# One program in place of two looped phases, in an attention and MLP block on one core

## The chip, the cores and the metric

The kernel runs on one core of a Trainium2 chip, in a single launch. The metric is device time in microseconds (us) of one execution. Shorter is better.

## What is computed

The input is 16 sequences of 256 tokens with 256 features, 4096 tokens in all. The reference, cut to what matters:

```python
x = x + layernorm(attention(layernorm(x), W_Q, W_K, W_V, W_O, biases))   # causal, 16 heads of 128
x = x + layernorm(mlp(layernorm(x), gate, up, down))                     # 2048 wide
# mlp: out = (gelu(x @ Wg.T) * (x @ Wu.T)) @ Wd.T
# Wg, Wu, Wd: two 4-bit codes in each word, a table of 16 values, one scale for 32 values
```

Every float32 product is computed as three matmuls of split operands (`hi` is the operand rounded to the matmul's type, `lo` the rest): hi by hi, hi by lo, lo by hi.

## The kernel before

The 4096 tokens are worked on in 8 chunks of 512. There are two phases, each with its own set of five engine programs (a `Block`), its own semaphores and its own SBUF and PSUM tensors: `attention_phase` for all chunks, then `mlp_phase` for all chunks. The second phase's programs begin when all engines have ended the first's. Each chunk's attention result goes through a scratch tensor in HBM (`x1_scratch`) to the MLP phase.

**Attention.** A chunk has 16 steps, one for each head; `step_plan(j)` writes out the order of the work of step j, and every engine walks the same list. In step j TensorE projects q and k of head j+1 (`project`, 6 matmuls of 512 columns each), transposes the probabilities of head j (`pT`, lines 465 to 467), projects v for four heads in every fourth step, multiplies head j-1's z by W_O (`out`, 12 matmuls of 256 columns), computes the scores of head j+1 and z of head j. ScalarE and VectorE take each result out of PSUM, as its hi and its lo part. In step 14 the next chunk's normalised x is transposed (`xT`, line 382), and q, k and scores "of head 16" are those of the next chunk's head 0. The last chunk does this too: its next chunk is the first one of the MLP phase for `xT`, and for q, k and scores there is no use.

The 16 steps are the body of a hardware loop over the chunks on every engine (`Fori`, on TensorE at line 418), so places in semaphore counts are register values:

```python
            with pe.Fori(0, NCH) as c:
                base = c * FPC
                for j, what in order:
```

At the end of the body come z of head 15, the scores of "head 16" and `out` of head 15. VectorE then evacuates the two output banks with the bias added (line 680).

The heads' weights (12.6 MB as hi and lo) stay in SBUF for the whole phase. The MLP weights are unpacked on the side, 6 of 48 pieces in each chunk: ScalarE starts loads of `words` and `scale` (lines 318 and 320), VectorE turns the codes into values (lines 583 to 599), ScalarE and GpSimd split them, and ScalarE stores hi and lo in an HBM scratch (line 308).

**MLP.** At its start SyncE loads the unpacked weights into SBUF (`w4all`, 12.6 MB, 18 transfers from line 842), since the memory was full of attention's. A chunk has 16 steps of 128 hidden columns. The work runs two steps ahead: step j has gate and up of step j+2 (`gate_up`, 12 matmuls of 512 columns, lines 925 to 927) and then `down` of step j (12 matmuls of 256 columns). ScalarE squares the gate (line 888), VectorE forms the argument (1049), ScalarE takes tanh (892), VectorE forms the product (1055 and 1058), ScalarE its hi part (897), GpSimd its lo part (1103); `down` of the step waits for both. Steps 14 and 15 of a chunk compute gate and up of the next chunk's steps 0 and 1 ("16" and "17"), and step 13 transposes its x (line 935). The first two are computed ahead of the loop. The last chunk computes "16" and "17" and the transposes too, on what the memory holds:

```python
                        if m == NT:
                            pe.wait_ge(s_xT_lo, c * KT + KT)
                        elif m == NT + 1:
                            pe.wait_ge(s_inter, base + NT)
```

While a chunk's matmuls run, VectorE finishes the chunk before (norm, residual) and normalises the next one. After the last `down`, ScalarE evacuates the result (918), VectorE and GpSimd normalise it (996, 1002, 1007, 1099), VectorE adds the residual (1024) and SyncE stores it.

Of the kernel before, what the change touches and what calls it, by code (L numbers as in the profile page):

```python
# [11 lines left out]
P = 128  # L27
# [21 lines left out]

class Tally:  # L50
# [10 lines left out]

PAIRS = [pair for h in range(0, HEADS, HG) for pair in (
    (("q", h), ("k", h)), (("v", h), ("v", h + 1)), (("v", h + 2), ("v", h + 3)),
    (("q", h + 1), ("k", h + 1)), (("o", h), ("o", h + 1)), (("q", h + 2), ("k", h + 2)),
    (("q", h + 3), ("k", h + 3)), (("o", h + 2), ("o", h + 3)))]


class Shared:  # L70


    def __init__(self, nc, ctx):
        def sb(name, shape, dt=F32):
            return ctx.enter_context(nc.sbuf_tensor(name, shape, dt))

        self.ident = sb("ident", [P, P])
        self.power = sb("power", [P, TT])

        self.stream = sb("stream", [P, TT, D])  # L80
        self.x_res = sb("x_res", [P, TT, D])
        self.xnT = [sb(f"xnT_{s}", [P, KT, CHUNK], F32R) for s in ("hi", "lo")]


def attention_phase(nc, shared, x_v, w_pairs, bq, bk, bv, bo, words_v, scales_v, x1_v, w4_v):

    with ExitStack() as ctx:
        def sb(name, shape, dt=F32):
            return ctx.enter_context(nc.sbuf_tensor(name, shape, dt))

        def sem(name):
            return ctx.enter_context(nc.semaphore(name))


        wqk_p = [sb(f"wqk_{s}", [P, HEADS, 2, KT, E], F32R) for s in ("hi", "lo")]
        wv_p = [sb(f"wv_{s}", [P, HEADS, KT, E], F32R) for s in ("hi", "lo")]
        wo_p = [sb(f"wo_{s}", [P, HEADS, D], F32R) for s in ("hi", "lo")]
        RAW = 2
        raw = sb("w_raw", [P, RAW, 2, D])
        bias_q = sb("bias_q", [P, HEADS])  # L100
        bias_k = sb("bias_k", [P, HEADS])
        bias_v = sb("bias_v", [P, HEADS])
        bias_o = sb("bias_o", [P, D])
        mask = sb("mask", [P, SEQ])
        ident, power = shared.ident, shared.power
        x_in = sb("x_in", [P, TT, D])
        x_res = shared.x_res
        xn = shared.stream
        xnT = shared.xnT
        qT = [[sb(f"qT{i}_{s}", [P, CHUNK], F32R) for s in ("hi", "lo")] for i in range(2)]  # L110
        k_both = [sb(f"kT{i}", [P, 2, CHUNK], F32R) for i in range(2)]
        kT = [[k[:, s, :] for s in range(2)] for k in k_both]
        v = [sb(f"v_{s}", [P, TT, HG * E], F32R) for s in ("hi", "lo")]
        probs = [sb(f"probs{b}", [P, 384]) for b in range(2)]
        pT = [[sb(f"pT{b}_{s}", [P, 384], F32R) for s in ("hi", "lo")] for b in range(2)]
        zT = [sb(f"zT_{s}", [P, CHUNK], F32R) for s in ("hi", "lo")]

        words = sb("words", [P, P], I32)
        spread = sb("spread", [P, P], I32)
        scale = sb("scale", [P, P])  # L120
        w4 = sb("w4", [P, 2, P])
        w4_p = [[sb(f"w4_{i}{s}", [P, 2, P], F32R) for s in ("hi", "lo")] for i in range(2)]
        nmax = [[sb(f"nmax{i}{b}", [P, 2]) for b in range(2)] for i in range(2)]
        sums = [[sb(f"sums{i}{b}", [P, 2]) for b in range(2)] for i in range(2)]
        rsum = [[sb(f"rsum{i}{b}", [P, 2]) for b in range(2)] for i in range(2)]
        stats = sb("stats", [P, TT, 6])
        mv = sb("mv", [P, TT, 2])
        var_eps = sb("var_eps", [P, TT])
        rstd = sb("rstd", [P, TT])
        token = sb("token", [P, 2])  # L130

        FB, UB = 3, 3
        fbank = [ctx.enter_context(nc.psum_tensor(f"fbank{i}", [P, 512], F32)) for i in range(FB)]
        ubank = [ctx.enter_context(nc.psum_tensor(f"ubank{i}", [P, 512], F32)) for i in range(UB)]
        obank = [ctx.enter_context(nc.psum_tensor(f"obank{i}", [P, 2, D], F32)) for i in range(2)]

        s_w = [sem(f"w_loaded{i}") for i in range(RAW)]
        s_w_split = sem("w_split")
        s_bias = sem("bias_loaded")
        s_words = sem("words_loaded")  # L140
        s_w4 = sem("w4_dequantised")
        s_w4_hi = sem("w4_hi")
        s_w4_lo = sem("w4_lo")
        s_w4_stored = sem("w4_stored")
        s_const = sem("const_ready")
        s_x = sem("x_loaded")
        s_xres = sem("x_res_loaded")
        s_res_used = sem("residual_added")
        s_stored = sem("x1_stored")
        s_var = sem("variance_ready")  # L150
        s_rstd = sem("rstd_ready")
        s_pool = sem("pool_chain")
        s_xn = sem("xn_ready")
        s_full = sem("full_ready")
        s_hi = sem("full_hi")
        s_lo = sem("full_lo")
        s_scores = sem("scores_ready")
# [1022 lines left out]
```

## Time and profile before

| | |
|---|---|
| median of 3 runs | 1764.58 us (1763.77 to 1765.21) |
| profiled execution | span 1763.2 us from the first to the last instruction; the page lists no time of its own beside it |
| attention phase, TensorE's first to last matmul | 10.84 to 1193.3 us |
| MLP phase, TensorE's first to last matmul | 1199.74 to 1752.3 us |
| TensorE matmul busy, share of the span | 1708.1 us, 97% |
| mean granted TensorE clock | 0.989 of full speed |

Busy time is what an engine spends in its own instructions; a releaser is the instruction that ended a wait. Where the releaser is "issue", the trace shows nothing that the engine waited for. Because matmuls are pipelined, the times from one start to the next tell their pace, not the duration of one.

### The profile page before, as it was taken

The numbers are of one execution on the slowest core, as the hardware profiler recorded it, in microseconds if no ns is written. First come the engines' busy times: TensorE is split into PE (matmuls) and PEld (weight loads), VectorE is DVE, ScalarE is ACT, GpSimd is POOL, SyncE is SP. The second block draws the span as 40 slices with busy tenths as digits, with TensorE's granted clock in tenths as the row PEclk, the third lists the DMA queues.
The fourth block names the chain that finished last, engine by engine and source line by source line (L and its number), as shares of the span: only waits on it lengthen the run. The fifth ranks groups of instructions, "written<-read, shape, count | busy, mean of one in ns | idle before, by whom it ended". The sixth has DMA issues, their size and how long they took to land. (4 is left out here: it accounts for less than half of the span.)

```text
span 1763.2 us, 34744 instructions
## 1 busy us (share of the span) xinstructions
PE 1708.1 (97%) x10678; PEld 1529.0 (87%) x10678; DVE 1233.6 (70%) x3538; ACT 933.5 (53%) x2290; POOL 524.9 (30%) x837
## 2 busy tenths in 40 slices
PE   6999999999999999999999999997999999999997
PEld 5998899899899889989989988996888888888886
DVE  5886787778688678777868867875665566566665
ACT  4665666556566566655656656563444444444443
POOL 6761222222122122222212212222333333333332
PEclk9999999999999999999999999999999999999999
DMA  4230010011001001001100100107100100100100
GB/s 120 82 104 22 14 50 30 12 46 37 3 22 50 22 14 50 30 12 46 37 3 22 50 22 14 51 18 298 36 24 12 36 24 12 36 24 12 36 24 12
DMA packets 62427, 69.02 MB, mean 39 GB/s; under 512 B 4776, under 2 KB 55848, under 8 KB 62248
## 3 DMA queue, kind: packets, MB, share of 16 engines
q1 hardware_dynamic: 34704, 47.87, 8.4%
q10 hardware_dynamic: 27544, 19.02, 3.4%
q8 instruction: 81, 1.33, 0.3%
q14 instruction: 98, 0.80, 0.1%
HBM read 45.38 MB, written 21.50 MB: 38 GB/s over the span
## 5 line engine op out<-in xcount | busy, mean ns | idle before, releaser
L719 POOL TENSOR_SCALAR probs<-probs,rsum 128x128 f32<-128x128 f32 (+1 forms) x516 | 218.4, 436 | 767.2 <-DVE rsum L532 758.9
L1103 POOL TENSOR_TENSOR iT_lo<-inter,iT_hi 128x512 fp32r<-128x512 f32 x129 | 166.4, 1290 | 331.0 <-ACT iT_hi L897 331.0
L292 ACT ACTIVATE probs<-probs,nmax 128x128 f32<-128x128 f32 x258 | 101.8, 395 | 256.6 <-DVE nmax L524 256.6
L364 PE MATMUL fbank<-xnT_hi,wqk_hi 128*128 128x512 f32 x516 | 215.8, 418 | 17.7 <-issue 16.3
L888 ACT ACTIVATE sq<-gbank 128x512 f32<-128x512 f32 x130 | 77.8, 598 | 278.1 <-PE gbank L927 278.1
L366 PE MATMUL fbank<-xnT_hi,wqk_lo 128*128 128x512 f32 x516 | 208.7, 405 | 0.0
L365 PE MATMUL fbank<-xnT_lo,wqk_hi 128*128 128x512 f32 x516 | 206.0, 399 | 0.0
L1049 DVE SCALAR_TENSOR_TENSOR th<-sq,gbank 128x512 f32<-128x512 f32 x130 | 89.3, 687 | 115.4 <-ACT sq L888 113.5
L1055 DVE SCALAR_TENSOR_TENSOR inter<-th,gbank 128x512 f32<-128x512 f32 x130 | 89.4, 687 | 99.7 <-ACT th L892 99.7
L364 PE MATMUL obank<-wo_hi,zT_hi 128*128 128x256 f32 x512 | 151.8, 297 | 2.8 <-DVE zT_lo L511 2.8
L925 PE MATMUL dbank<-w4all_hi,iT_hi 128*128 128x256 f32 x512 | 144.9, 283 | 0.0
L927 PE MATMUL dbank<-w4all_hi,iT_lo 128*128 128x256 f32 x512 | 144.9, 283 | 0.0
L926 PE MATMUL dbank<-w4all_lo,iT_hi 128*128 128x256 f32 x512 | 144.8, 283 | 0.0
L366 PE MATMUL obank<-wo_hi,zT_lo 128*128 128x256 f32 x512 | 143.2, 280 | 0.0
L365 PE MATMUL obank<-wo_lo,zT_hi 128*128 128x256 f32 x512 | 142.9, 279 | 0.0
L365 PE MATMUL fbank<-pT_lo,v_hi 128*128 128x256 f32 (+1 forms) x512 | 142.7, 279 | 0.0
L366 PE MATMUL fbank<-pT_hi,v_lo 128*128 128x256 f32 (+1 forms) x512 | 142.1, 278 | 0.0
L364 PE MATMUL fbank<-pT_hi,v_hi 128*128 128x256 f32 (+1 forms) x512 | 137.4, 268 | 2.4 <-DVE v_lo L509 2.0
L509 DVE TENSOR_TENSOR v_lo<-fbank,v_hi 128x512 fp32r<-128x512 f32 x128 | 88.6, 692 | 72.2 <-ACT v_hi L282 72.2
L283 ACT ACTIVATE kT<-fbank,bias_k 128x512 fp32r<-128x512 f32 x129 | 88.8, 688 | 88.8 <-PE fbank L366 88.8
L511 DVE SCALAR_TENSOR_TENSOR kT<-fbank,bias_k,kT 128x512 fp32r<-128x512 f32 x129 | 96.8, 751 | 50.6 <-ACT kT L283 49.5
L364 PEld LDWEIGHTS fbank<-xnT_hi,wqk_hi 128*128 128x128 f32 x516 | 100.4, 195 | 36.2 <-issue 17.7
(124 smaller groups left out, 5352.3 us busy)
## 6 DMA issues: line engine op xcount, KB each, us to landing
w_raw<-in_w_pairs SPq DMA_DIRECT2D x32, 256.0 KB, 2.7
w4all_hi<-w_hi_scratch SPq DMA_DIRECT2D x7, 768.0 KB, 15.0
w4all_lo<-w_lo_scratch SPq DMA_DIRECT2D x7, 768.0 KB, 16.9
x_res<-in_x SPq DMA_DIRECT2D x9, 512.0 KB, 5.4
x_scratch<-stream SPq DMA_DIRECT2D x9, 512.0 KB, 3.9
x_in<-x_scratch SPq DMA_DIRECT2D x9, 512.0 KB, 3.8
x_in<-in_x SPq DMA_DIRECT2D x8, 512.0 KB, 3.5
x_res<-x_scratch SPq DMA_DIRECT2D x8, 512.0 KB, 4.6
```

Of the source, the lines that this page charges most:

```text
L292: act.activation(pr[:, 0:P], pr[:, 0:P], ACT.Exp, bias=nmax[i][b][:, 0:1], scale=-1.0, accum_out=sums[i][b][:, 0:1])
L364: nc.tensor.matmul(out, a[0], b[0], start=start, stop=False, skip_group_check=skip)
L365: nc.tensor.matmul(out, a[0], b[1], start=False, stop=False, skip_group_check=skip)
L366: return nc.tensor.matmul(out, a[1], b[0], start=False, stop=stop, skip_group_check=skip)
L511: ins = dve.scalar_tensor_tensor(dst, bank, bias, hi.bitcast(F32), ALU.add, ALU.subtract)
L719: last = pool.tensor_scalar(probs[b][:, lo:hi], probs[b][:, lo:hi], rsum[i][b][:, part:part + 1], 1.0, ALU.mult, ALU.mult)
L925: nc.tensor.matmul(out, a[0], b[0], start=start, stop=False, skip_group_check=skip)
L926: nc.tensor.matmul(out, a[0], b[1], start=False, stop=False, skip_group_check=skip)
L927: return nc.tensor.matmul(out, a[1], b[0], start=False, stop=stop, skip_group_check=skip)
L1049: dve.scalar_tensor_tensor(th[j % 2][:], sq[j % 2][:], 1.0 / GELU_A, gbank[slot(j)][:], ALU.add, ALU.mult).then_inc(s_arg, 1)
L1055: after(dve.scalar_tensor_tensor(act_v[j % 2][:], th[j % 2][:], 1.0, gbank[slot(j)][:], ALU.add, ALU.mult), loop)
L1103: pool.tensor_tensor(iT[j % 4][1][:], act_v[j % 2][:], iT[j % 4][0][:].bitcast(F32), ALU.subtract).then_inc(s_iT_lo, 1)
```

## The change

The two phases become one set of five engine programs (`load_program`, `scalar_program`, `tensor_program`, `vector_program`, `pool_program`) in one `Block`, with one set of semaphores and memory.

- All loops over chunks are unrolled. The order lists `STEPS` and `MLP_STEPS` carry the chunk as well; all places in semaphore counts are constants.
- The attention weights of q, k and v and the MLP weights share one tensor, `weights`. In the last attention chunk SyncE loads the MLP weights over those of heads that are done (`load_w4`), in eight parts of 1.5 MB.
- The last attention step has gate and up of the MLP's steps 0 and 1 where it had q, k and scores of a chunk that doesn't exist. MLP banks are the attention banks under other names, and MLP tiles lie in attention's (`iT` in q and k, `act_v` in the probabilities, `th` in the raw weights' buffer).
- The last MLP chunk computes no gate and up of a next chunk and transposes no x for it. In chunk 0 of attention the norm and residual of "the chunk before" are left out, and of the 49 loads of `words` and `scale` 48 are left.
- `square` writes to `th` itself, and the next chunk's x is normalised in place in `x_in`; its load now waits for the transposes of the one before.

```diff
-            with pe.Fori(0, NCH) as c:
-                base = c * FPC
-                for j, what in order:
+    for c, j, kind, m in STEPS:
...
+def step_plan(c, j):
+    last = c == NCH - 1 and j == HEADS - 1
+    plan = [("gu", 0)] if last else [("q", j + 1), ("k", j + 1)]
...
+    return plan + [("z", j), ("gu", 1) if last else ("scores", j + 1), ("out", j)]
...
+def mlp_plan(c, j):
+    ahead = [("gu", j + 2)] if c < NCH - 1 or j + 2 < NT else []
+    if j == NT - 3:
+        return ahead + ([("xT", 0)] if c < NCH - 1 else []) + [("down", j)]
+    if j == NT - 2:
+        return [("down", j)] + ahead
+    return ahead + [("down", j)]
...
+    def load_w4(q):
+        last = (6 * q + 5) // 2
+        sp.wait_ge(s.full, nth(("k", NCH - 1, min(last, HEADS - 1), 0)))
+        if last >= HEADS:
+            sp.wait_ge(s.full, nth(("v", NCH - 1, TT - 1, HEADS // HG - 1)))
+        sp.wait_ge(s.w4_stored, 32 * (6 * q + 6))
+        for part in range(2):
+            sp.dma_start(mem.w4_all[part][:, 6 * q:6 * q + 6].bitcast(F32),
+                         w4_v[part][:, 6 * q:6 * q + 6]).then_inc(s.w4_all[q], 16)
...
+    next_x(NCH - 1, chunk(x1_v, 0))
+    load_w4(0)
+    load_w4(1)
+    finish(NCH - 1)
+    for q in range(2, NT // 2):
+        load_w4(q)
...
+        elif kind == "gu":
+            if m == 0:
+                pe.wait_ge(s.lo, nth(("xT", c, KT - 1, 0)))
+            pe.wait_ge(s.lo, before_in_bank(GATES[m]))
+            pe.wait_ge(s.pT_lo, 2 * HEADS * NCH - 2 + m)
+            gate_up(m)
...
-        attention_phase(nc, shared, x_v, w_pairs, bq, bk, bv, bo, words, scales, x1_v, w4_v)
-        mlp_phase(nc, shared, x1_v[:, TT:, :], w4_v, out_v)
+        mem, s = Memory(nc, ctx), Signals(nc, ctx)
+        block = ctx.enter_context(nc.Block())
```

TensorE before, from the end of the attention loop's body over the branch back and out of the phase to the first gate of the MLP phase:

```order
1057 L364 MATMUL obank<-wo_hi,zT_hi 128x256
1058 L365 MATMUL obank<-wo_lo,zT_hi 128x256
1059 L366 MATMUL obank<-wo_hi,zT_lo 128x256
1060 L418 REGISTER_ALU
1061 L418 COMPARE_AND_BRANCH
1062 L87 UNCONDITIONAL_BRANCH
1063 L921 UNCONDITIONAL_BRANCH [waits barrier_Pool_Activation_PE_DVE_SP_release]
1064 L925 MATMUL gbank<-xnT_hi,w4all_hi 128x512 [waits w4_first_loaded]
```

TensorE in the changed kernel, the same place: the last chunk's z of head 15 ends, gate and up of step 1 begin (12 matmuls), `out` of head 15, and gate and up of step 2:

```order
7202 L490 MATMUL fbank<-pT_hi,v_lo 128x128
7203 L488 MATMUL fbank<-xnT_hi,weights 128x512 [waits pT_lo,full_lo]
...
7214 L490 MATMUL ubank<-xnT_hi,weights 128x512
7215 L488 MATMUL obank<-wo_hi,zT_hi 128x256 [waits full_lo]
...
7226 L490 MATMUL obank<-wo_hi,zT_lo 128x256
7227 L488 MATMUL fbank<-xnT_hi,weights 128x512 [waits w4_loaded1,pT_lo,full_lo]
```

The branches and the barrier are gone, and the wait for the first weights now stands in one row with waits that the attention steps had.

TensorE before, the end of the MLP loop's body, with gate "17" ahead of the last `down`; this body also ends the program:

```order
1469 L965 REGISTER_ALU
1470 L925 MATMUL gbank<-xnT_hi,w4all_hi 128x512 [waits inter_ready]
...
1481 L927 MATMUL hbank<-xnT_hi,w4all_lo 128x512
1482 L925 MATMUL dbank<-w4all_hi,iT_hi 128x256 [waits inter_lo,inter_hi]
...
1494 L954 REGISTER_ALU
1495 L954 COMPARE_AND_BRANCH
```

TensorE in the changed kernel, its last 37 rows: `down` of steps 13, 14 and 15 stand one behind the other.

```order
10259 L490 MATMUL ubank<-xnT_hi,weights 128x512
10260 L488 MATMUL obank<-weights,qT 128x256 [waits inter_lo,inter_hi]
...
10272 L488 MATMUL obank<-weights,kT 128x256 [waits inter_lo,inter_hi]
...
10284 L488 MATMUL obank<-weights,kT 128x256 [waits inter_lo,inter_hi]
...
10296 L1012 UNCONDITIONAL_BRANCH
```

Ahead of the last `down` there is now no other matmul between it and the step before it.

## Rows read from the trace of the kernel before

**Rows 1.** The page: busy us (share of the span) and instructions by engine.

```profile
PE 1708.1 (97%) x10678; PEld 1529.0 (87%) x10678; DVE 1233.6 (70%) x3538; ACT 933.5 (53%) x2290; POOL 524.9 (30%) x837
```

**Rows 2.** TensorE's waits: engine, tile and line, releaser; us in total, times, longest.

```profile
PE fbank L364 <- issue: 16.3, 7, 2.6
...
PE gbank L925 <- DMA w4all_lo<-w_lo_scratch: 8.6, 3, 6.2
```

**Rows 3.** Timeline of TensorE at the second branch back (start us, us, instruction).

```profile
310.49 0.39 PE L364 MATMUL obank<-wo_hi,zT_hi 128*128 128x256 f32 x1 [0.34 <-DVE zT_lo L511]
...
311.89 0.28 PE L366 MATMUL obank<-wo_hi,zT_lo 128*128 128x256 f32 x1
314.47 0.49 PE L364 MATMUL fbank<-xnT_hi,wqk_hi 128*128 128x512 f32 x1 [2.30 <-issue]
...
318.92 0.27 PE L465 MATMUL ubank<-ident,probs 128*128 128x128 f32 x1
```

**Rows 4.** Stretch behind it: PE, PEld, DVE, ACT, POOL, PEclk, DMA share, GB/s.

```profile
314.50:319.00 4.50, 4.50 (x13) 3.50 (x14) 0.75 (x2) 0.69 (x1) 0.00 (x0) 0.62 0.04 9
```

**Rows 5.** Seven stretches, `out` of head 15 to the next pT: PE, PEclk, DMA, GB/s.

```profile
163.80:172.15 8.35, 6.11 (x25) 0.80 0.03 9
...
sum 59.04, PE 42.76; mean PE 6.11
```

**Rows 6.** Timeline of TensorE, one q and k projection inside a chunk.

```profile
1183.59 0.45 PE L364 MATMUL fbank<-xnT_hi,wqk_hi 128*128 128x512 f32 x1
...
1186.40 0.27 PE L465 MATMUL ubank<-ident,probs 128*128 128x128 f32 x1
```

**Rows 7.** Timeline of TensorE where the MLP loop branches back, twice.

```profile
1277.23 0.28 PE L927 MATMUL dbank<-w4all_hi,iT_lo 128*128 128x256 f32 x1
1277.35 0.40 PE L925 MATMUL gbank<-xnT_hi,w4all_hi 128*128 128x512 f32 x1
...
1345.18 0.40 PE L925 MATMUL gbank<-xnT_hi,w4all_hi 128*128 128x512 f32 x1
```

**Rows 8.** Queues' packets, MB, share: one of 165 to 312 us, all of 1260 to 1760.

```profile
q8 instruction: 10, 0.16, 0.4%
...
q1 hardware_dynamic: 10717, 10.63, 6.9%
```

**Rows 9.** Timeline of TensorE from one phase to the other.

```profile
1190.09 0.33 PE L391 MATMUL ubank<-kT,qT_hi 128*128 128x256 f32 x1
...
1199.74 0.79 PE L925 MATMUL gbank<-xnT_hi,w4all_hi 128*128 128x512 f32 x1 [6.24 <-DMA w4all_lo<-w_lo_scratch]
...
1212.28 0.28 PE L925 MATMUL dbank<-w4all_hi,iT_hi 128*128 128x256 f32 x1
```

**Rows 10.** TensorE in the last chunk: gate and up "15", the transposes, `down` 15.

```profile
1738.63 0.40 PE L925 MATMUL gbank<-xnT_hi,w4all_hi 128*128 128x512 f32 x1
...
1741.38 0.63 PE L935 MATMUL gbank<-ident,x1n 128*128 128x128 f32 x4
...
1750.68 0.28 PE L925 MATMUL dbank<-w4all_hi,iT_hi 128*128 128x256 f32 x1
```

**Rows 11.** VectorE, ScalarE and GpSimd at the end of the last chunk.

```profile
1743.02 0.69 DVE L1058 SCALAR_TENSOR_TENSOR inter<-inter,hbank 128x512 f32<-128x512 f32 x1
...
1750.33 0.63 ACT L897 ACTIVATE iT_hi<-inter 128x512 fp32r<-128x512 f32 x1 [0.21 <-DVE inter L1058]
...
1751.04 1.29 POOL L1103 TENSOR_TENSOR iT_lo<-inter,iT_hi 128x512 fp32r<-128x512 f32 x1 [1.75 <-ACT iT_hi L897]
```

**Rows 12.** A stretch of the weights' load, columns as in rows 4.

```profile
1203.00:1215.00 12.00, 9.68 (x47) 7.60 (x46) 6.58 (x11) 4.43 (x8) 2.56 (x2) 1.00 1.01 417
```

**Rows 13.** Timeline of the side work: codes' load issued, their first use.

```profile
1144.04 0.37 ACTq L318 DMA_DIRECT2D words<-in_words  x1
...
1154.72 0.22 DVE L583 TENSOR_SCALAR spread<-words 128x128 int32<-128x128 int32 x1
```

**Rows 14.** DMA issues between 1193 and 1260 us: count, KB each, us to landing.

```profile
x_in<-x_scratch SPq DMA_DIRECT2D x2, 512.0 KB, 12.7
```

More of the change, by code:

```diff
@@ new lines, in __init__, with bank @@
+        self.var_eps = sb("var_eps", [P, TT])
+        self.rstd = sb("rstd", [P, TT])
+        raw = self.raw[:].rearrange("p a b d -> p (a b d)")
+        self.th = [raw[:, i * CHUNK:(i + 1) * CHUNK] for i in range(2)]
+        self.act_v = [rows[:, i * CHUNK:(i + 1) * CHUNK] for i in range(2)]
+        self.iT = [*self.qT, *self.kT]
+        def bank(name, shape):
+            return ctx.enter_context(nc.psum_tensor(name, shape, F32))
+        self.fbank = [bank(f"fbank{i}", [P, 512]) for i in range(FB)]
@@ L91, in sem, with __init__ @@
+        self.ubank = [bank(f"ubank{i}", [P, 512]) for i in range(UB)]
+        self.obank = [bank(f"obank{i}", [P, 2, D]) for i in range(2)]
+        units = 2 * HEADS * NCH
+        first, second = (GATES[i] % FB for i in range(2))
+        self.gbank = [self.fbank[i] for i in (first, second, 3 - first - second)]
+        self.hbank = [self.ubank[(units + 1 + i) % UB] for i in (-1 + UB, 0, 1)]
+class Signals:
+    def __init__(self, nc, ctx):
         def sem(name):
             return ctx.enter_context(nc.semaphore(name))
-        wqk_p = [sb(f"wqk_{s}", [P, HEADS, 2, KT, E], F32R) for s in ("hi", "lo")]
@@ new lines, in __init__ @@
+        self.w = [sem(f"w_loaded{i}") for i in range(RAW)]
+        self.w_split = sem("w_split")
+        self.bias = sem("bias_loaded")
+        self.const = sem("const_ready")
+        self.words = sem("words_loaded")
+        self.w4 = sem("w4_dequantised")
+        self.w4_hi = sem("w4_hi")
+        self.w4_lo = sem("w4_lo")
+        self.w4_stored = sem("w4_stored")
+        self.w4_all = [sem(f"w4_loaded{q}") for q in range(NT // 2)]
+        self.x = sem("x_loaded")
+        self.xres = sem("x_res_loaded")
@@ new lines, in __init__ @@
+        self.pT = sem("pT_ready")
+        self.pT_hi = sem("pT_hi")
+        self.pT_lo = sem("pT_lo")
+        self.out = sem("out_ready")
+        self.out_used = sem("out_evacuated")
+        self.dve = sem("dve_chain")
+        self.pool = sem("pool_chain")
+        self.xT = sem("x1nT_ready")
+        self.xT_hi = sem("x1nT_hi")
+        self.xT_lo = sem("x1nT_lo")
+        self.gate = sem("gate_ready")
+        self.up = sem("up_ready")
+        self.sq = sem("square_ready")
+        self.arg = sem("tanh_argument_ready")
@@ new lines, in __init__, with x1_norm, next_norm, y_norm @@
+        self.tanh = sem("tanh_ready")
+        self.inter = sem("inter_ready")
+        self.iT_hi = sem("inter_hi")
+        self.iT_lo = sem("inter_lo")
+        self.down = sem("down_ready")
+        self.down_used = sem("down_evacuated")
+        self.y = sem("y_ready")
+        self.yres = sem("y_res_loaded")
+        self.y_stored = sem("y_stored")
+def x1_norm(c):
+    return 2 * c + 1
+def next_norm(c):
+    return 2 * c + 2
+def y_norm(c):
+    return 2 * NCH + 2 * c + (1 if c < NCH else 0)
```

1593 lines of the change are left out of this document (720 added, 873 removed).

## The prediction

> **What bounds the kernel now.** I read the page first: TensorE is busy 1708.1 of 1763.2 us, VectorE 70%, the others less [rows 1]. A busy TensorE need not be at its best, so the timeline of its starts comes next: inside a chunk each matmul starts as soon as the array has taken the one before, and no other engine sets the pace. The change can win only in TensorE's path, in three ways: instructions that are not issued, time in which it stands, and time at a lower clock. Then I read its waits, which tell where it stands. Beside the start there are two large kinds: seven waits of 16.3 us in all with no releaser ("issue"), and three of 8.6 us on the load of the MLP weights [rows 2]. The timeline shows where they lie. The seven stand where the attention loop branches back, one for each of the seven returns to its head; at the second the last `out` matmul starts at 311.89 and q's first at 314.47 [rows 3]. The three stand at the start of the MLP phase. The stretches by time add what the waits don't tell: behind a branch back the granted clock is 0.62 of full, which is a mix of the two levels, 2.4 and 1.2 GHz; before it fell, TensorE had stood for 2.30 us [rows 3, 4]. So a branch costs more than its gap.
>
> **Part 1, no branch back in attention: 28.7 us.** Measured from the start of `out` of head 15 to the start of the next probabilities' transposes (pT), the seven stretches take 59.04 us in all [rows 5]. At full clock the work in one is `out`, 310.49 to 311.89 and 0.12 for the last matmul, 1.52 us [rows 3], and one projection of q and k, 1183.59 to 1186.40, 2.81 us [rows 6]: 4.33 us, seven times 30.3. The rest, 28.7 us, is gap and low clock, 4.1 us for each. I count all of it as gained, for in straight code TensorE goes from `out` to q with nothing to wait for: q of head 1 reads the transposed x of step 14, and its bank was evacuated long ago. What hides no cost but could come next is VectorE, which evacuates the output banks just there; the banks that v needs are those of q and k, and pT and a first v (about 2 us) lie between. If that cover were gone, the evacuation of 1.3 us would show at most seven times, 9 us.
>
> Is the gap the branch's? At the MLP loop's branch the last `down` starts at 1277.23 and the next gate at 1277.35, the pace of a matmul: no gap [rows 7]. What differs is the instruction stream: in one attention chunk a queue fetches ten packets of instructions, 0.16 MB, while from 1260 to 1760 us, seven MLP chunks, the only queue at work is one of data [rows 8]. So I read it that the MLP body is held, and that attention's jump back waits for code. The Trainium skill ("Advanced Engine Details and Errata", Control Flow Timing) prices a compare-and-branch at about 108 ns; by that the seven would be worth 0.8 us, and the forecast 28 us higher. The MLP loop agrees with it, the attention loop does not. The skill's "Runtime: NRT & Kernel Launch", Instruction fetch mechanics, says that a taken branch to code outside the held window must fetch it first, which agrees with both loops.
>
> **Part 2, MLP loops unrolled: 0 us.** There is no gap to win [rows 7]. The body now streams its code once for each chunk. Ten packets came in without one "issue" gap inside attention's chunk, and by the code the MLP chunk has 392 matmuls in 67.8 us (1277.35 to 1345.18) [rows 7] where attention has 936 in 146.7 (163.80 to 310.49) [rows 3, 5], less per us. I take 0; the bound above is the rival below, and below 0 lies nothing, as there is no gap.
>
> **Part 3, from one phase to the other: 15.2 us.** Before, from the end of the last z (scores begin at 1190.09) to the first `down` (1212.28) pass 22.2 us [rows 9]: scores for an absent head, `out`, the barrier and first load (6.24 us of standing), three times gate and up, the first of them at the lower clock, and two more waits on the load. After, the same stretch holds gate and up 1, `out` and gate and up 2. Gate and up take 1738.63 to 1741.38, 2.75 us [rows 10]; 2.75 + 1.5 + 2.75 = 7.0. Gained 15.2. Gate and up 0 take the place of q and k of the absent head, 2.75 for 2.81: 0.1, dropped.
>
> The new waits there are met in time. Gate 0 wants the transposed x, as q did. `out` of head 15 wants zT's lo part; it stood 0.34 us for it behind 1.2 us of scores and now has 2.75 us of cover, so that wait goes too (inside the 15.2). `down` 0 wants GpSimd's lo part of step 0's product: the chain square, argument, tanh, product, hi, lo is some 6 us of instructions, and between gate 0 and `down` 0 lie some 12 us. It also wants the output banks evacuated, 1.3 us of VectorE behind `out`, covered by gate and up 2. The MLP weights come in parts of 1.5 MB in the last chunk, 3.8 us each at the 417 GB/s of the old load [rows 12]; the last part can start in step 14 and is first read by gate 14, twelve steps of 4.2 us later.
>
> **Part 4, the load inside the last attention chunk: 0 us, up to 15.** It shares the DMA engines with the codes' loads. These have 1144.04 to 1154.72, 10.7 us, from issue to first use [rows 13]. While the whole load ran, a 512 KB transfer took 12.7 us to land [rows 14], 2 us over that, and 3 with the second transfer's issue behind the first's; five such loads fall in the last chunk, and if all were late by 3 us and VectorE's delay passed to TensorE whole, it would be 15 us. But a part is 3.8 us of traffic, not 30, and VectorE is 70% busy: I take 0 and keep 15 for the range. Instruction packets could be late likewise; in the old burst TensorE showed no "issue" wait.
>
> **Part 5, the end: 4.8 us.** Gate and up "16" and "17" (5.5 us) and eight transposes (0.9) go. The last `down` began at 1750.68 [rows 10]. Now gate and up 15 end at 1741.38, `down` 13 and 14 follow until 1744.2, and `down` 15 must wait for its operand: the product is done at 1743.71, its hi part takes 0.63, its lo part 1.29 [rows 11], with hand-overs some 1745.8. So a wait of 1.6 us takes the place of cover, and 1750.7 - 1745.9 = 4.8 us are gained. Behind it the evacuation, norm, residual and store are the same as before.
>
> **Sum.** 28.7 + 0 + 15.2 + 0 + 4.8 = 48.7 us. The profiled span of 1763.2 becomes 1714.5. The median of the runs shown is 1764.58, 1.4 above the span; with the same 1.4, the time is 1716 us. The start, 10.8 us until the first normalised x, is untouched.
>
> **Rivals.**
> *The gap is not the branch's* (a wait that the trace doesn't show, such as a count at the loop's head). Then part 1 stays and only parts 3 and 5 are won: 1764.6 - 20 = 1745 us. For it: the releaser is blank, and the MLP loop has none. Against: seven returns, seven gaps of 2.1 to 2.6 us, and none at the first entry. It is also what the skill's 108 ns would make of the change. Chance 5%.
> *The load in the last chunk or late evacuations are felt*: 5 to 15 us of part 4 or 9 of part 1 come back, 1721 to 1731. For it: SyncE's queue was crowded in the old burst. Chance 11%.
> *Slower: straight code starves TensorE in the MLP.* Its loop ran from held instructions; now each chunk fetches. By the ratio of matmuls, 392 to 936, it is 4.2 packets a chunk, 33 in all, and if each came as late as behind a branch, 4.1 us, this costs 135 us: 1716 + 135 = 1851. It decides from 12 late packets on (49 over 4.1). Against: attention's body takes ten a chunk at a higher rate, with a gap at the branch alone. Chance 3%.
> *The change gains more*: the smaller waits on v's and z's lo parts (0.2 to 0.3 us, 15 in all) shrink with fewer register instructions on VectorE and ScalarE, or the start is a little shorter: up to 5 us, 1711. Chance 6%.
>
> **How the numbers follow.** My forecast, 1716 us, has 75%. The range holds it, the larger gain and most of the felt load: 1711 to 1731. It leaves out the branch rival, the slower one and a small rest. A measurement of this kernel can tell 0.2%, 3.5 us, from no change. Only the slower rival is on that side, 3%, and a mishap of exactly the gain's size has 1%: faster 0.96, same 0.01, slower 0.03.
>
> **What would show it.** In the profile after, no "issue" wait at a chunk's start and a granted clock of 1.00 there; from one `out` of head 15 to the next 142.7 us for 146.9. No stretch without matmuls between attention and MLP. MLP chunks of 67.8 us as before; a longer one with "issue" waits speaks for the slower rival. One wait of TensorE on `iT`'s lo part, 1.6 us, ahead of the last `down`. In the last attention chunk, no wait of VectorE on `words`. The sum is wrong if the seven gaps remain, or if TensorE's matmuls in the last chunk keep a slower pace.

## The result, and the profile after

| | before | changed kernel |
|---|---|---|
| median | 1764.61 us (1763.77 to 1765.21) | 1725.8 us (1724.96 to 1726.8) |
| profiled execution, span | 1763.2 us | 1723.1 us |
| mean granted TensorE clock | 0.989 | 0.998 |

The ratio is 0.978, with a 95% interval of 0.977 to 0.980. The forecast was 1716.0 us, with a range of 1711 to 1731: the direction and the range held, and the gain was 40.1 us of span where 48.7 were forecast. By the medians 9.8 us are missing. Of these, 8.6 are span in the profiled execution; 0.8 is that this execution was the fastest of its four, and 0.4 that its time is 1.9 us above its span, where the forecast's is 1.5 above. The 8.6 us are the subject of most of what follows.

The page's busy times of the changed kernel, and the queues (packets, MB, share), to be read beside [rows 1] and [rows 8]:

```profile
PE 1690.0 (98%) x10624; PEld 1506.7 (87%) x10624; DVE 1210.9 (70%) x3488; ACT 928.3 (54%) x2273; POOL 518.3 (30%) x825
...
q8 instruction: 85, 1.39, 0.3%
q14 instruction: 58, 0.48, 0.1%
```

The page counts 54 matmuls fewer, and TensorE is still the bound. Its waits over the whole span (line, releaser; us in total, times, longest), where [rows 2] had "issue" and the weights' load:

```profile
PE fbank L504 <- DVE stream L700: 12.3, 1, 12.3
PE obank L488 <- DVE zT_lo L669: 2.4, 7, 0.3
PE fbank L488 <- DVE v_lo L667: 2.3, 8, 0.3
PE ubank L510 <- DVE kT L669: 1.6, 1, 1.6
PE fbank L488 <- DVE xnT_lo L667: 1.4, 1, 1.4
PE obank L488 <- POOL kT L990: 1.4, 1, 1.4
```

Both large kinds are gone. What is left is the start, which has grown (10.8 to 12.3 us), two waits of 1.6 and 1.4 us in the first steps, which the kernel before has as well, some of 0.3 us, and one of 1.4 us on GpSimd ahead of the last `down`. The place of [rows 3], TensorE from one chunk to the next, now reads:

```profile
308.35 0.39 PE L488 MATMUL obank<-wo_hi,zT_hi 128*128 128x256 f32 x1 [0.34 <-DVE zT_lo L669]
...
309.76 0.28 PE L490 MATMUL obank<-wo_hi,zT_lo 128*128 128x256 f32 x1
309.88 0.40 PE L488 MATMUL fbank<-xnT_hi,weights 128*128 128x512 f32 x1
...
312.68 0.82 PE L581 MATMUL ubank<-ident,probs 128*128 128x128 f32 x6
```

From the last `out` to the first q pass 0.12 us, the pace of a matmul, where 2.58 us had passed. The stretch from `out` to pT takes 4.33 us here and 4.26 to 4.33 in all seven chunks; part 1 put 4.33 for its work. The stretch behind it is at full clock (PE, PEld, DVE, ACT, POOL, PEclk, DMA share, GB/s), where [rows 4] had 0.62:

```profile
308.40:317.00 8.60, 8.60 (x46) 7.34 (x47) 6.10 (x20) 5.20 (x14) 1.65 (x4) 1.00 0.00 0
```

From attention to MLP, where [rows 9] had 22.2 us from the last z to the first `down`:

```profile
1165.32 0.45 PE L488 MATMUL fbank<-xnT_hi,weights 128*128 128x512 f32 x1
...
1168.16 0.28 PE L488 MATMUL obank<-wo_hi,zT_hi 128*128 128x256 f32 x1
...
1169.57 0.40 PE L488 MATMUL fbank<-xnT_hi,weights 128*128 128x512 f32 x1
...
1172.38 0.28 PE L488 MATMUL obank<-weights,qT 128*128 128x256 f32 x1
```

Gate and up 1, `out` of head 15, gate and up 2 take 7.06 us (7.0 forecast), with no wait in them. But a small thing can be read here: gate and up are 2.81 us (1169.57 to 1172.38), where they were 2.75 [rows 10]. The last attention chunk, which has the load, beside the one before it, in the columns of [rows 4]:

```profile
1024.20:1168.20 144.00, 143.71 (x939) 129.62 (x940) 110.40 (x362) 86.76 (x234) 34.10 (x75) 1.00 0.32 115
881.10:1024.20 143.10, 142.41 (x937) 128.49 (x937) 109.25 (x361) 85.67 (x232) 34.05 (x74) 1.00 0.09 29
```

Four times the traffic, TensorE busy for 143.71 of 144.00 us, and 0.9 us more, of which gate and up 1 in the place of the scores are 1.0: the load costs nothing there. The end, as forecast, has one wait on the lo part (1.36 us for 1.6):

```profile
1710.39 0.36 PE L488 MATMUL obank<-weights,kT 128*128 128x256 f32 x1 [1.36 <-POOL kT L990]
```

### Where the 8.6 us are

Four cuts of TensorE's timeline, before and after, each against the sum of the parts that falls in it:

| stretch | before | after | gained | forecast |
|---|---|---|---|---|
| to `out` of head 15, last chunk | 1191.82 | 1168.16 | 23.7 | 27.7 |
| from there to the first `down` | 20.46 | 4.22 | 16.2 | 16.2 |
| first `down` to last `down` | 538.40 | 538.01 | 0.4 | 4.8 |
| last `down` to the end | 12.52 | 12.71 | -0.2 | 0 |

(The 27.7 is part 1 less the 1.0 us of gate and up 1 ahead of `out`, which part 3 has back.) The transition is exact. The first and the third stretch lack 4.0 and 4.4 us. In the first, 1.5 are the later start: 12.32 for 10.84. The rest is pace: the attention chunks follow each other at 143.1 us, forecast 142.7; those of the MLP at 68.4, where they were 67.8 and should have stayed so. (The gain of part 5 can be seen beside it: from the first `down` of the last chunk to the last one pass 59.2 us where 63.6 had passed.) One MLP step of the kernel before, then of the changed one (`down`, gate, next `down`):

```profile
1424.11 0.28 PE L925 MATMUL dbank<-w4all_hi,iT_hi 128*128 128x256 f32 x1
...
1425.54 0.40 PE L925 MATMUL gbank<-xnT_hi,w4all_hi 128*128 128x512 f32 x1
...
1428.29 0.28 PE L925 MATMUL dbank<-w4all_hi,iT_hi 128*128 128x256 f32 x1
```

```profile
1424.05 0.28 PE L488 MATMUL obank<-weights,kT 128*128 128x256 f32 x1
...
1425.46 0.40 PE L488 MATMUL fbank<-xnT_hi,weights 128*128 128x512 f32 x1
...
1428.26 0.28 PE L488 MATMUL obank<-weights,qT 128*128 128x256 f32 x1
```

Nothing waits in either. Gate and up went from 2.75 to 2.80 us, `down` from 1.43 to 1.41. Each matmul of 512 columns takes some 3 to 4 ns more, each `down` 1 to 2 ns less, and there are some 3060 of the first kind. The clock was full in both, and the instructions are the same; what differs is where their operands lie in memory. In the kernel before xnT lies ahead of the weights, in the changed one behind them.

### The profile page after: what moved, and what is told of

It is laid out like the page before. It is cut to its first block, busy times and chain, and to the rows that moved or that the text cites. A ratio compares the mean times of both kernels' runs of the same rounds, so it can differ in the third digit from the quotient of the medians.

```text
span 1723.1 us, 29141 instructions
## 1 busy us (share of the span) xinstructions
PE 1690.0 (98%) x10624; PEld 1506.7 (87%) x10624; DVE 1210.9 (70%) x3488; ACT 928.3 (54%) x2273; POOL 518.3 (30%) x825
## 4 chain that ended last, share of the span: by engine, by line
PE 97%; DVE 1%; ACT 1%; issue 0%; POOL 0%; DMA 0%; POOLq 0%; DVEq 0%; ACTq 0%
PE fbank L488 17%; PE fbank L490 17%; PE fbank L489 17%; PE obank L488 7%; PE obank L489 7%; PE obank L490 7%; PE ubank L488 6%; PE ubank L489 5%; PE ubank L490 5%; PE ubank L581 5%; PE ubank L510 2%; PE ubank L513 1%; PE fbank L504 1%; DVE v_lo L667 0%; DVE zT_lo L669 0%; DVE stream L700 0%
## 5 line engine op out<-in xcount | busy, mean ns | idle before, releaser
L488 PE MATMUL fbank<-xnT_hi,weights 128*128 128x512 f32 x768 | 310.5, 404 | 1.4 <-DVE xnT_lo L667 1.4
L490 PE MATMUL fbank<-xnT_hi,weights 128*128 128x512 f32 x768 | 304.4, 396 | 0.0
L489 PE MATMUL fbank<-xnT_lo,weights 128*128 128x512 f32 x768 | 303.9, 396 | 0.0
L404 ACT ACTIVATE w_raw<-fbank 128x512 f32<-128x512 f32 x128 | 76.5, 597 | 265.2 <-PE fbank L490 265.2
L490 PEld LDWEIGHTS fbank<-xnT_hi,weights 128*128 128x128 f32 x768 | 144.5, 188 | 34.6
L488 PEld LDWEIGHTS fbank<-xnT_hi,weights 128*128 128x128 f32 x768 | 145.1, 189 | 25.4 <-DVE xnT_lo L667 1.8
L777 DVE SCALAR_TENSOR_TENSOR w_raw<-w_raw,fbank 128x512 f32<-128x512 f32 x128 | 87.9, 687 | 111.7 <-ACT w_raw L404 111.6
L489 PEld LDWEIGHTS fbank<-xnT_lo,weights 128*128 128x128 f32 x768 | 145.2, 189 | 23.8
L783 DVE SCALAR_TENSOR_TENSOR probs<-w_raw,fbank 128x512 f32<-128x512 f32 x128 | 87.9, 687 | 97.6 <-ACT w_raw L408 97.6
L990 POOL TENSOR_TENSOR qT<-probs,qT 128x512 fp32r<-128x512 f32 x64 | 82.9, 1295 | 176.5 <-ACT qT L413 176.5
L669 DVE SCALAR_TENSOR_TENSOR zT_lo<-fbank,bias_v,zT_hi 128x512 fp32r<-128x512 f32 x128 | 96.1, 750 | 50.5 <-ACT zT_hi L372 50.4
```

Source lines behind the costliest of these rows:

```text
L488: nc.tensor.matmul(out, a[0], b[0], start=start, stop=False, skip_group_check=skip)
L489: nc.tensor.matmul(out, a[0], b[1], start=False, stop=False, skip_group_check=skip)
L490: return nc.tensor.matmul(out, a[1], b[0], start=False, stop=stop, skip_group_check=skip)
L669: ins = dve.scalar_tensor_tensor(dst, bank, bias, hi.bitcast(F32), ALU.add, ALU.subtract)
L777: dve.scalar_tensor_tensor(mem.th[j % 2], mem.th[j % 2], 1.0 / GELU_A, mem.gbank[slot(j)][:], ALU.add, ALU.mult).then_inc(s.arg, 1)
L783: after(dve.scalar_tensor_tensor(act_v, mem.th[j % 2], 1.0, mem.gbank[slot(j)][:], ALU.add, ALU.mult))
```

## The experiments

Twelve kernels were run in three sets. In each set the kernel before was timed as well, with a median between 1764.3 and 1764.6 us; so differences of a few us between kernels can be read.

### The branch back: e1 and e8

The kernel before, with only TensorE's attention loop unrolled:

```diff
-            with pe.Fori(0, NCH) as c:
+            for c in range(NCH):
```

> The kernel before, with TensorE's attention loop alone unrolled; the other engines keep their loops. Theory (the jump back fetches code, and the clock falls in the gap): the seven gaps of 2.1 to 2.6 us and the half-clock matmuls behind them go, 28.7 us less, 1764.6 - 28.7 = 1736 us, and from one out of head 15 to the next 143 us. Rival (a wait that the trace does not show, or the other engines' branches hold TensorE): the gaps stay, 1764 us. Part-way, around 1745 to 1755, would mean that VectorE's or ScalarE's own branch back is late next.

Measured: 1749.0 us (1747.94 to 1749.59), ratio 0.991 (0.989 to 0.993). The gain is 15.6 us, not 28.7. The seven waits without a releaser are gone, so the gap was the branch's. The instruction queues tell more. The pages of the kernel before and, behind the dots, of e1 (packets, MB, share):

```profile
q8 instruction: 81, 1.33, 0.3%
q14 instruction: 98, 0.80, 0.1%
...
q8 instruction: 64, 1.05, 0.3%
q14 instruction: 98, 0.80, 0.2%
```

Only q8 changed with TensorE's loop, so it carries TensorE's code, and 17 packets fewer were fetched. At the second return of the kernel before, from 311 to 315 us, q8 brought two packets:

```profile
q8 instruction: 2, 0.03, 3.8%
```

The whole chunk, 165 to 312 us, has ten, and e1 has none from 309 to 313, where its own second chunk ends. So code is fetched at the jump back, as the prediction read it, though no run changes the fetch alone. The waits now name another releaser (columns as above):

```profile
PE fbank L364 <- DVE qT_lo L511: 10.5, 7, 1.6
```

On the timeline one of them stands behind the first six v matmuls of a chunk:

```profile
606.39 0.50 PE L364 MATMUL fbank<-wv_hi,xnT_hi 128*128 128x512 f32 x1 [1.64 <-DVE qT_lo L511]
```

VectorE still branches back, and evacuates q late, so that v has no bank. This is the place that part 1 named as the next to be late (the banks of q and k that v needs). If that is the rest of the 28.7, it goes with VectorE's loop. The kernel before, with TensorE's and VectorE's attention loops unrolled (shown is VectorE's):

```diff
...
-            with dve.Fori(0, NCH) as c:
+            for c in range(NCH):
                 base = c * FPC
-                loop = c * per_step
+                loop = None
...
```

> The kernel before with TensorE's and VectorE's attention loops unrolled. With TensorE's alone (e1) the gaps of 2.1 to 2.6 us went, but a wait of 1.4 to 1.65 us for VectorE's lo part of q came in at most chunks, and 15.6 us were gained of 28.7. Theory (VectorE's own jump back makes it late): that wait goes too, 1736 to 1738 us. Rival (the evacuation of the output banks makes VectorE late, not its jump): the wait stays, 1749 us; ScalarE's jump as the next one late would show as a wait of VectorE on ScalarE's hi part there, around 1740 to 1745.

Measured: 1735.93 us (1735.09 to 1737.3), ratio 0.984 (0.982 to 0.986). The gain over before is 28.4 us; part 1 had 28.7. In the profiled execution, too, 28.4 us are gained from TensorE's first matmul to the last `out` of head 15, and the chunks follow each other at 142.8 us; 1.6 us more are gained from there to the first `down`, where TensorE waits 6.1 us on the MLP weights for 8.6. The wait on `qT_lo` is not in its list, and q14 has 71 packets for 98. So part 1 needs both engines' branches away, and ScalarE's and GpSimd's were worth next to nothing here: they were still loops in this kernel.

### Straight code in the MLP: e2

The same edit at TensorE's MLP loop alone (line 954).

> The kernel before, with TensorE's MLP loop alone unrolled. After the change a 512-column matmul of the MLP takes 233 ns from start to start where most took 227 before, and a step 4.21 us for 4.18. Theory A (the operands' new places in SBUF set the pace): here the places are the old ones, so 227 ns and 4.18 us a step, 1764.6 us unchanged. Theory B (code that streams in sets the pace): 233 ns, 4.21 us a step, 4 to 5 us more, 1769 us.

Measured: 1764.51 us (1763.69 to 1765.36), ratio 1.000 (0.999 to 1.001), and the pace of the MLP's matmuls unchanged. Code was streamed in this run: from 1260 to 1760 us q8 brought 22 packets, where the kernel before has none. So neither the branch nor streaming the code costs anything there that can be measured, and the rival by which straight code starves TensorE falls. It also falls as an explanation of the slower pace in the changed kernel.

### Where xnT lies: e3, e5, e6, e7

The changed kernel with `stream`, `x_res` and `xnT` allocated ahead of the weights, and nothing else:

```diff
...
+        self.stream = sb("stream", [P, TT, D])
+        self.x_res = sb("x_res", [P, TT, D])
+        self.xnT = [sb(f"xnT_{s}", [P, KT, CHUNK], F32R) for s in ("hi", "lo")]
...
-        self.x_res = sb("x_res", [P, TT, D])
-        self.stream = sb("stream", [P, TT, D])
-        self.xnT = [sb(f"xnT_{s}", [P, KT, CHUNK], F32R) for s in ("hi", "lo")]
```

> The changed kernel with stream, x_res and xnT placed ahead of the weights in SBUF, at the very addresses that they had before; nothing else. Theory A (places): up's matmuls at 227 ns again and the MLP step near 4.18 us, v's first matmul too, so 4 to 7 us less than 1725.8: 1719 to 1722. Theory B (streaming code): no difference, 1725.8.

Measured: 1713.3 us (1712.99 to 1713.73), ratio 0.971 (0.969 to 0.973): 12.5 us less than the changed kernel, from an edit that changes no instruction but its addresses. A step of it:

```profile
1169.96 0.28 PE L488 MATMUL obank<-weights,qT 128*128 128x256 f32 x1
...
1171.37 0.40 PE L488 MATMUL fbank<-xnT_hi,weights 128*128 128x512 f32 x1
...
1174.10 0.28 PE L488 MATMUL obank<-weights,qT 128*128 128x256 f32 x1
```

Gate and up 2.73, `down` 1.41: neither is slower than in the kernel before (2.75 and 1.43) or in the changed one (2.80 and 1.41). The attention chunk is now 142.75 us, for the 142.7 of the forecast, and the MLP chunk 67.2, which is less than the 67.8 of before. That is why the edit gains more than the placement had cost.

Is it the region (ahead, behind) or the exact address? Listing the tensors' offsets in a partition shows that the move also changed xnT's offset modulo 128 bytes from 96 to 32, with the weights at 32 in both. Three kernels tell these apart. In e5 xnT stays behind the weights and is moved by 64 bytes, and q, k, v and z, which lie behind it, move along:

```diff
+        self.pad = sb("pad", [P, 16])
```

> The changed kernel with 64 bytes of padding ahead of x_in, so that xnT and all behind it move up by 64 bytes; the weights stay. In the changed kernel weights start at byte 18080 of a partition (32 over a multiple of 128) and xnT at 166752 (96 over one); in e3, 12.5 us faster, xnT starts at 25248 (32 over) and the weights at 34464 (32 over). Theory A1 (the place within 128 bytes counts, or that both operands stand alike in it): both are 32 over now, so 512-column matmuls at 227 ns for 233 and 1713 to 1716 us. Theory A2 (which region of SBUF counts, in front or behind): no change, 1725.8 us.

In e6 xnT is in front as in e3, and the same pad is ahead of all of it, so every offset moves by 64 and the relations stay:

> e3 with 64 bytes of padding ahead of stream: xnT at 25312 and the weights at 34528, both 96 over a multiple of 128, both in front. Theory A1 as 'the place within 128 bytes': slow again, 233 ns, about 1725. Theory A1 as 'both alike': fast, 1713. Theory A2 (region): fast, 1713.

In e7, again with xnT in front, the small tensors (8 bytes each) are sorted so that every large one starts at a multiple of 128:

> e3 with five small tensors moved so that xnT, the weights, q, k, v, the probabilities and z all start at multiples of 128 bytes. If the place within 128 bytes counts, full alignment may be best of all: the matmuls still at 231 to 233 ns in e3 (gate's, and two in three of q's and k's) go to 227 too, 5 us less than e3, 1708. If only the region counts, 1713 as e3.

Measured: e5 1716.42 us (1714.59 to 1716.74), e6 1713.47 (1713.14 to 1713.83), e7 1716.59 (1715.23 to 1716.7). The table has the offsets modulo 128 and the pace: the mean time from one start to the next, from the timelines, over all matmuls of the kind (some 3050, 1530 and 1530; intervals over 300 ns left out, as most of them hold a wait).

| kernel | xnT, weights | gate, up, q, k: ns | weights, `iT` | `down`: ns | W_O, zT | `out`: ns | median us |
|---|---|---|---|---|---|---|---|
| before | 32, 32 | 232.0 | 32, 32 | 119.8 | 32, 96 | 123.7 | 1764.6 |
| changed | 96, 32 | 235.4 | 32, 96 | 118.2 | 32, 96 | 123.5 | 1725.8 |
| e3 | 32, 32 | 231.3 | 32, 96 | 118.2 | 32, 96 | 123.6 | 1713.3 |
| e5 | 32, 32 | 230.8 | 32, 32 | 120.0 | 32, 32 | 124.6 | 1716.4 |
| e6 | 96, 96 | 231.4 | 96, 32 | 118.2 | 96, 32 | 123.6 | 1713.5 |
| e7 | 0, 0 | 230.7 | 0, 0 | 120.0 | 0, 0 | 124.6 | 1716.6 |
| e12 | 32, 96 | 235.6 | 96, 96 | 119.4 | 96, 32 | 123.6 | 1771.5 |

(e12 is the kernel of the next section.) One regularity holds in all seven: the 512-column matmuls of gate, up, q and k are fast (231 to 232) where both operands start alike modulo 128, and slow (235.4 to 235.6) where they are 64 bytes apart; `down` and `out`, of 256 columns, are the other way round, by 1 to 2 ns. The same 3060 matmuls at 235.4 and at 231.3 ns differ by 12.5 us, the size of e3's gain. The projection of v, also 512 columns wide, reads the same two tensors with their parts exchanged and shows it more weakly: 227.5 to 228.7 ns alike, 229.2 apart. The region doesn't matter (e5), nor the offset itself (e6, e7). The Trainium skill ("SBUF — State Buffer", Who interferes with whom) says of TensorE that it has two independent read ports, one for the moving operand and one for the weights, and that it never waits on anyone. Both statements are about one engine beside another. The runs show that the places of its own two operands, taken together, change its pace by up to 2%. Why it is so isn't shown.

### The same regularity on the kernel before: e12

If the regularity is not an accident of the changed kernel, it must be possible to make the old one slower by it, with 64 unused bytes of each partition between xnT and the weights:

```diff
...
+        self.pad = sb("pad", [P, 16])
...
```

> The kernel before with 64 unused bytes of each partition between xnT and the weights, so that the two no longer start alike modulo 128 bytes in attention and MLP. Theory (their relative start sets the pace of the matmuls that read both): some 3060 matmuls of 512 columns go from 231 to 234.5 ns, +10.7 us, while down and out, of 256 columns, gain 1 to 2 ns each on some 3000, -3 to -5 us: 1769 to 1775 us. Rival (it is another property of the changed kernel's memory, not the relative start): 1764.4 within 1 us.

Measured: 1771.53 us (1771.0 to 1772.01), ratio 1.004 (1.002 to 1.005), slower by 7.0 us. The pace of the 512-column matmuls is the slow one, and a step takes 4.23 us for the 4.18 above:

```profile
1426.88 0.28 PE L926 MATMUL dbank<-w4all_hi,iT_hi 128*128 128x256 f32 x1
...
1428.30 0.40 PE L926 MATMUL gbank<-xnT_hi,w4all_hi 128*128 128x512 f32 x1
...
1431.11 0.28 PE L926 MATMUL dbank<-w4all_hi,iT_hi 128*128 128x256 f32 x1
```

From the first `down` to the last that is 7.0 us (545.4 for 538.4), all of what was measured: 1.1 us lost up to the last `out` of head 15 and 1.1 gained between the phases cancel. Only 0.3 of the 1.1 us came in attention from the first to the last `out` of head 15, though a step there is slower too. The windows behind the branches back tell why (PE busy and count, PEclk, DMA share, GB/s); these are the first, second and fifth of seven:

```profile
164.30:172.60 8.30, 5.48 (x22) 0.79 0.03 8
311.80:320.00 8.20, 5.29 (x31) 1.00 0.03 8
...
752.30:760.60 8.30, 5.89 (x33) 1.00 0.03 8
```

In two of the seven the clock did not fall behind the gap, and these stretches from `out` to pT take 7.2 and 6.7 us for 8.4 to 8.7. That gives back some 3 us. It was not foreseen. The length of the gap alone doesn't decide it: the two are the longest of the seven and the shortest, 2.66 and 2.13 us, and what does isn't settled.

### The start: e4

In the changed kernel TensorE starts at 12.32. VectorE's four instructions that normalise the first x, with GpSimd beside them:

```profile
8.04 4.13 DVE L700 TENSOR_SCALAR stream<-x_in,mv,rstd 128x256 f32<-128x256 f32 x4 [1.52 <-POOL rstd L942]
```

```profile
8.09 0.62 POOL L973 TENSOR_SCALAR weights<-w_raw 128x512 fp32r<-128x512 f32 x1
8.79 1.26 POOL L975 TENSOR_TENSOR weights<-w_raw,weights 128x512 fp32r<-128x512 f32 x1
10.02 0.66 POOL L973 TENSOR_SCALAR weights<-w_raw 128x512 fp32r<-128x512 f32 x1
```

The four took 3.00 us in the kernel before, where GpSimd's first one began 0.13 us after VectorE's; now it is 0.05. Before, VectorE's first took 0.41 us and GpSimd's 0.76 for 0.62; now VectorE's takes 0.82 and GpSimd's 0.62. The other three of VectorE's take 0.7 to 1.4 us in both kernels. To test the contention, GpSimd waits for the normalised x before it splits weights:

```diff
+    pool.wait_ge(s.xn, 1)
```

> The changed kernel with one wait more: GpSimd begins to split the heads' weights only when VectorE has normalised the first x. In the changed kernel's trace three of VectorE's four instructions of that step take 0.8 to 1.4 us, each ending as a GpSimd instruction ends, where one took 0.41 before. Theory (the two engines hold each other up at SBUF): the four take about 0.4 us each, 1.6 to 2.0 in all for 4.13, and TensorE starts at 10 us for 12.3; but the first weights are split 2 us later, at about 12, which its first projection at 13.5 still meets: 2.3 us less, 1723.5. Rival (no contention, slow instructions at the start): no gain, or a loss of up to 2 us by the later weights.

Measured: 1723.84 us (1723.66 to 1724.22), ratio 0.977 (0.976 to 0.979), 2.0 less than the changed kernel. The four instructions take 1.38 us:

```profile
8.24 1.38 DVE L700 TENSOR_SCALAR stream<-x_in,mv,rstd 128x256 f32<-128x256 f32 x4 [1.52 <-POOL rstd L942]
```

GpSimd begins to split 1.6 us later (9.71 for 8.09), and VectorE ends 2.55 us earlier (9.62 for 12.17): work that had time stood in the way of work on the path. The Trainium skill ("SBUF — State Buffer", Who interferes with whom) states that a VectorE instruction in a two-port mode, which a `tensor_scalar` can enter, and a GpSimd instruction shut each other out for a whole instruction. The trace agrees in that VectorE's four take 4.13 against 1.38 us; it doesn't show the mode.

### The load and the absent gates: e10 and e11

Both start from e3. In e10 every part of the MLP weights waits for z of head 14 of the last chunk:

```diff
     def load_w4(q):
...
+        sp.wait_ge(s.full, nth(("z", NCH - 1, HEADS - 2, 0)))
...
-    load_w4(0)
-    load_w4(1)
     finish(NCH - 1)
-    for q in range(2, NT // 2):
+    for q in range(NT // 2):
```

> From the kernel with xnT ahead of the weights, 1713.3 us. All eight parts of the MLP weights are loaded only behind z of head 14 in the last attention chunk. Theory (the gain at the transition needs the load to lie under attention's matmuls): gate 0 then stands for the first part of 1.5 MB, about 3.8 us at 417 GB/s and 2 us until it lands, less the 1 to 2 us between z of head 14 and gate 0, and its matmuls behind the stand run at the lower clock; the last part lands some 31 us later, by when gate 14 is not yet due. 1719 to 1723 us, 1721 taken. Rival (the place of the load does not matter, the gain at the transition came from the barrier and the absent head alone): within 1 us of 1713.3.

Measured: 1721.78 us (1720.69 to 1722.07), 8.5 above e3. TensorE stands once, and behind it the clock is 0.53:

```profile
1163.38 0.77 PE L487 MATMUL fbank<-xnT_hi,weights 128*128 128x512 f32 x1 [6.46 <-DMA weights<-w_lo_scratch]
```

```profile
1163.40:1168.00 4.60, 4.60 (x12) 3.63 (x13) 0.69 (x1) 0.60 (x1) 0.00 (x0) 0.53 1.01 421
```

The stand of 6.46 us, and 5.40 us from gate 0 to the next `out` where e3 has 3.39 (1156.81 to 1160.20), are 8.5 us. So of part 3's 15.2 us some 8.5 hang on the load's place under attention's matmuls, which the memory shared with the heads' weights allows. By the prediction's reckoning the rest is the absent head's scores, one gate and up fewer in the stretch, and the barrier; no run takes these apart.

In e11 the last MLP chunk has gate and up "16" and "17" again, without the transposes; one wait of TensorE and the places of ScalarE's and GpSimd's last parts are set to fit:

```diff
-    ahead = [("gu", j + 2)] if c < NCH - 1 or j + 2 < NT else []
+    ahead = [("gu", j + 2)]
...
```

> From the kernel with xnT ahead of the weights, 1713.3 us. The last MLP chunk computes gate and up 16 and 17 of an absent chunk again (24 matmuls of 512 columns), ahead of down 14 and of down 15, and no transposes. Theory: 24 matmuls at 0.229 to 0.231 us are 5.5 us, and the 1.36 us that TensorE stands ahead of the last down goes, as it has cover again: +4.1 us, 1717.4 (1716.9 to 1718.0). Rival (matmuls cost their whole time, the wait stays): +5.5 us, 1718.8. Second rival (the end is not set by TensorE): 1713.3.

Measured: 1716.96 us (1716.56 to 1717.23), 3.7 above e3. From `down` 13 to `down` 15 pass 8.45 us (1693.97 to 1702.42) where e3 has 4.49, which is 3.96 for the 4.1 expected, and the wait ahead of the last `down` is gone. Part 5's reckoning, cover for a wait against matmuls, holds.

### Both repairs: e9

The changed kernel with xnT in front (e3) and GpSimd's wait (e4).

> The changed kernel with both repairs: xnT laid ahead of the weights (1713.3 us alone) and GpSimd's splitting held back until x is normalised (2.0 us gained alone). If the two are independent, 1711.3 us (1710.8 to 1711.8). If the earlier start is taken up by another wait in this placement, 1713.3.

Measured: 1709.93 us (1709.62 to 1710.56), ratio 0.969 (0.968 to 0.971), which is 15.9 less than the changed kernel. Beside e3 it is 3.4 less, where e4 alone had brought 2.0 and 1711.3 us were expected of the two together. TensorE starts at 9.73 us, 2.79 before e3, and at the first `out` of head 15 it is 3.41 ahead. In e4 it starts 2.55 earlier and is 2.07 ahead there. The difference lies in the pace of the first matmuls: the first 20 are busy for 6.59 us in e9 and 7.21 in e3, for 6.86 in e4 and 6.41 in the changed kernel. Each is one execution, and what sets that pace wasn't tested.

## Why the prediction was right, and where it was short

**What bounds the kernel** was right: everything won or lost was in TensorE's path.

**Part 1, 28.7 us,** was right in size, 28.4 in e8, and in that the branch is the cause; the packets at the jump speak for the fetch of code. In the changed kernel the seven stretches take 4.26 to 4.33 us and the clock stays full. The sentence on what could come next, banks that v needs, named the place but not the reason: it put the evacuation of the output banks for it, and it was VectorE's own branch, which shows once TensorE's is gone (e1, 10.5 us of waits). As the change unrolls all engines, it didn't show. The rival that the gap is not the branch's is out. With it falls what the forecast had worked out from the Trainium skill's 108 ns ("Advanced Engine Details and Errata", Control Flow Timing): the MLP loop, where e2 won nothing, doesn't speak against that price, but the return of attention's long body costs 4.1 us.

**Part 2, 0 us,** was right (e2), and the slower rival falls; it had put 33 packets for the MLP, and 22 came in e2. The changed kernel fetched 85 and 58 packets of instructions on its two instruction queues in the whole span, and TensorE never waited for one.

**Part 3, 15.2 us,** was right to 0.1 us (15.1 by the timelines), **part 4, 0 us,** too: the last chunk is longer only by its gate and up. e10 shows what the place of the load was worth, 8.5 us.

**Part 5, 4.8 us,** was right in its mechanism: the wait was 1.36 us for 1.6, and e11 gave 3.7 back for two gates and ups of 5.5. In the changed kernel the last MLP chunk shows it, 4.4 us shorter up to its last `down`, while over all eight the slower pace took 4.4 us again.

**The sum** is the step that fell short. It said that the changed kernel is the old one less 48.7 us, and so took two things for unchanged:

- "MLP chunks of 67.8 us as before", and 142.7 for attention's. The diff moved the tensors in memory, and xnT came to lie 64 bytes off the weights modulo 128. That cost 0.5 us for each MLP chunk and 0.4 for each of attention's, some 7 us in all. The profile of before could not tell it, since there the two started alike; the diff told that the allocations moved, and the text gave that no price and no bound. As a term it would have needed its rows from a placement that no trace had.
- The start, "10.8 us until the first normalised x, is untouched". It became 12.3. The x came later, VectorE's first instruction on it at 4.57 us for 4.08, and 0.35 us of that is left when the normalising begins (8.04 for 7.69); this varies from run to run (e2, on the kernel before, has 4.48, and TensorE starts at 11.23). The other 1.1 us are the normalising, 4.13 us for 3.00, where GpSimd's splitting meets it.

Together 1.5 + 7 are the 8.6 us to within 0.2. The range held because it had room above for a felt load and late evacuations, neither of which occurred. So the gains came for the reasons given, and that the miss fell inside the range was luck: the room was kept for other things.

## What to carry to other kernels

A hardware loop cost nothing here with a body of 392 matmuls, for which no instruction packet came in, and 4.1 us for each return with one of 936 and ten packets, gap and low clock together. Read it off the timeline and the instruction queues at the branch, and look at every engine that loops, since the second one shows only when the first is gone. Work on absent chunks and a phase's first load are worth looking for at each seam; a load can go into memory whose owner is done, under the matmuls of the phase before. When an edit rearranges memory and TensorE bounds the kernel, compare the pace of its matmuls before and after, and try the two operands' starts alike and 64 bytes apart modulo 128: that is one line of code, and was worth 12.5 us here.

## What the runs showed of the hardware

- A matmul's pace depends on where its two SBUF operands start relative to each other: gate, up, q and k, of 512 columns, 231 to 232 ns alike and 235.4 to 235.6 at 64 bytes apart; `down`, of 256, 119.4 to 120.0 alike and 118.2 apart; `out` 124.6 alike and 123.5 to 123.7 apart. It was made to go in the changed kernel and to appear in the kernel before. The cause is open, and other distances than 0 and 64 weren't tried.
- At the return of attention's long loop body two packets of TensorE's code, 16 KB each, came in within 4 us, and TensorE stood for 2.1 to 2.6 us. The MLP's body returned without a packet or a gap, and straight code was never waited for.
- VectorE's branch back in attention costs TensorE 1.5 us each time (10.5 us in seven), in a place that TensorE's own return hides.
- Behind a gap of 2.1 to 2.6 us the granted clock fell seven times of seven in the kernel before, and in e12, with gaps of 2.1 to 2.7 us, five of seven. Behind e1's waits of some 1.5 us in attention it stayed full.
- GpSimd and VectorE, together at the start, lengthened VectorE's four instructions from 1.38 to 4.13 us.
